# Resident products in TensorE's waits of the first and the last element of a two-layer cross-attention

## The chip, the cores and the metric

One core of a Trainium2 chip. The metric is the device time of one execution in microseconds, the median of several runs.

## What is computed

32 elements (B = 32) pass through two layers of cross-attention with a residual each. An element has 112 queries of 320 channels and a context of 375 positions by 512 channels; there are 20 heads of 16. In the first layer the first 77 context positions ("text") and the rest ("image") have their own softmax and their own key and value weights:

```python
out_text = _merge_heads(_attend(q, k, v, sm_scale))
out_ip = _merge_heads(_attend(q, k_ip, v_ip, sm_scale))
out = (out_text + IP_SCALE * out_ip) @ Wo.T + bo + residual
```

In the second layer the first 371 positions are the text and the last 4 the image; the image scores get a cosine between the attention-weighted context and the four image positions, and a mask by query:

```python
qsem = _l2norm(jnp.einsum('bhst,bte->bhse', probs_t, text_ehs))
sem = jnp.einsum('bhse,bne->bhsn', qsem, ip_n)
probs_ip = softmax(attn_scores + SEM_SCALE * sem) * spatial_mask[None, None, :, None]
out = (text_out + ip_out) @ W_out + b_out + residual
```

## The kernel before, in words

Nothing is scheduled by a tool. `stage_order` (L53) writes one list of stages by hand, and each of the five engines walks through that same list (`tensor` L578, `vector` L837, `scalar` L1041, `gpsimd` L1214, `sync` L1291) and issues its own share of each stage, with waits on semaphores. So a stage's place in the list sets the order on every engine and on SP's DMA queue.

Large products are split in two or three parts of lower precision: keys, values and the Gram matrix of the context run as fp32r products of high and low parts (`k` L583, `v_mm` L651, `g` L666), scores as stacks of bfloat16 parts in one product (`scores` L698). To stay in range each query's maximum over the keys is found first: `s_max` (L677) makes the scores of 3 heads in `ST` (three PSUM banks) or of 2 heads in `PN` (the two banks `PV` and `NS`), VectorE reduces them (L930 to L936), `m_T` (L692) transposes the maxima, GpSimd splits them in three parts (`m_split` L1267), and six (or three) DMAs put them as extra rows into `Qs` (L1419), for which the first `scores` wait. The queries (`q`, L635) and the text keys (L587 to L593) are plain float32 products of 128 weights; a call of `e.matmul` on float32 leaves two records of MATMUL in the profile.

The keys and queries in their parts go to DRAM (`k` L1361, `q` L1397) and come back with the parts stacked (`k_stack` L1386, `q_stack` L1403).

PSUM has three more banks `R0` to `R2` that all small results take in turn: `in_bank` (L58) gives a result the next bank, and `free` (L554) makes TensorE wait until the one that had this bank three results ago was read.

For element b the loop (L286) issues the first layer of element b and the second layer of element b-1, and between them the keys, values and Gram tiles of element b+1, so that TensorE has work while ScalarE makes exponentials and VectorE multiplies. The first element (b = 0) has no second layer of an earlier one to fill its waits, and there the weights are loaded and split as well (`key_weights` L892, `weights` L897). In the last rounds (b = 31 and b = 32) no further element is there: the maxima of the second layer of element 31 (`maxima`, L354, `between` L340), the second layer of element 31 (`groups1` L161), and the chain at its end, `ns_T`, `fuse`, `ip_softmax`, `ip_T`, `ip_mm`, `o_T`, `o_mm`, `out` (`finish1` L204), where each step waits for the one before on another engine. `take` (L229) draws steps from these generators; `finish0` (L190) is the chain `pvT`, `o_T`, `o_mm`, `x1_T`, `q` that ends the first layer.

`wkt` (L406) holds the first layer's text key weights as float32, `[128, 4, 384]`; it is loaded once (L1304) and stays.

Of the kernel before, what the change touches and what calls it, by code (L numbers as in the profile page):

```python
# [6 lines left out]
B, S, C, T, E = 32, 112, 320, 375, 512  # L7
# [21 lines left out]
class Order:  # L29
# [15 lines left out]
    def share(self, buffer, slots, what, signal, value):  # L45
# [3 lines left out]
        self.freed[buffer, what] = ends[len(ends) - slots] if len(ends) >= slots else None  # L49
        ends.append((signal, value))  # L50


def stage_order():  # L53
    o = Order()
# [6 lines left out]
    def flush():  # L61
        now = later[:]
        later.clear()
        for stage in now:
            o.add(*stage)

    def keys(b, l, m):
        o.add("k", b, l, m)
        in_bank(("k", b, l, m), "k_rem", o.at("k", b, l, m))
        o.share("rem", 2, ("k", b, l, m), "k_low", o.at("k", b, l, m))  # L70
# [47 lines left out]
    def maxima(b, l, between):  # L118
        for h in range(0, H, 5):
            for h0, wide in ((h, True), (h + 3, False)):  # L120
                o.add("s_max", b, l, h0, wide)
                if wide:
                    o.share("ST", 1, ("s_max", b, l, h0), "s_max_read", o.at("s_max", b, l, h0, wide))
                else:
                    for part in ("PV", "NS"):
                        o.share(part, 1, ("s_max", b, l, h0), "s_max_read", o.at("s_max", b, l, h0, wide))
                between()
        return m_rows(b, l)
# [100 lines left out]
    def take(pieces, n):  # L229
        for _ in range(n):  # L230
            next(pieces, None)
# [7 lines left out]
    o.add("split", 0)  # L239
    o.add("key_weights", 0)  # L240
    keys(0, "t", 0)
    keys(0, 0, 0)
    o.add("image_keys")
    for m in range(3):
# [9 lines left out]
    o.add("k_stack", 0, 0, 0)  # L254
    o.add("k_stack", 0, 0, 1)
    o.add("q_stack", 0, 0)
    for m in range(2):
        keys(0, 1, m)
    o.add("ctx", 1)
# [1 line left out]
    in_bank("image_values", "vip_copied", 1)  # L261
    in_bank("image_norms", "nip_max", 1)
    o.add("vip_out")
    o.add("text_rest")
    o.add("v_mask")
    o.add("weights", 2)
# [5 lines left out]

    start = with_maxima()
    take(start, 3)
    rows0 = maxima(0, 0, lambda: take(start, 1))
    take(start, 99)
    flush()
    o.add("split", 1)
# [7 lines left out]
    for b in range(B + 1):  # L286
        if b + 1 < B:
            o.add("xT", b + 1)
        pieces = ahead(b) if b < B else iter(())
        first, last = iter(()), iter(())  # L290

        def among0(g):
            take(rows1, 1)
            take(pieces, 1 if b + 1 < B and (b or g < 4) else 0)
            if g < 2:
                flush()

        def among1(g, end):
            if g or not end:
                take(first, 1)  # L300
            if g == 0 and b + 1 < B:
                take(pieces, 1)
            if end and g == 2 and b < B:
                o.add("k_stack", b, 1, 0)

        if not b:
            take(pieces, 2)
        if b < B:
            groups0(b, among0)
            first = finish0(b)  # L310
        else:
            flush()
            flush()
        take(rows1, 9)
        if not b:
            take(pieces, 2)
        if b + 1 < B:
            o.add("k_stack", b + 1, 0, 0)
            o.add("k_stack", b + 1, 0, 1)
            o.add("q_stack", b + 1, 0)  # L320
        if b:
            groups1(b - 1, among1)
            last = finish1(b - 1)
            take(last, 1)
        else:
            o.add("k_stack", b, 1, 0)
        take(first, 99)
        if b < B:
            o.add("k_stack", b, 1, 1)
            o.add("q_stack", b, 1)  # L330
        if not b:
            take(pieces, 3)
        if b + 1 < B:
            o.add("xn", b + 1)
        if b + 2 < B:
            o.add("ctx", b + 2)
        count = [0]
        rows0 = iter(())

        def between():  # L340
            count[0] += 1
            if count[0] > 9:
                take(rows0, 1)
            if count[0] in (1, 2, 3, 5, 7, 9, 10):
                take(last, 1)
            if count[0] in (2, 4, 6, 8, 11, 12, 14, 16):
                take(pieces, 1)
        if b + 1 < B:
            rows0 = maxima(b + 1, 0, between)
            take(rows0, 1)  # L350
        if b + 1 == B:
            take(pieces, 99)
        if b < B:
            rows1 = maxima(b, 1, between)  # L354
            take(rows1, 1)
        take(rows0, 9)
        take(last, 99)
        take(pieces, 99)
    return o

# [24 lines left out]
def xattn_two_layers(nc, a, out):  # L385
# [3 lines left out]
    with ctx:  # L389
# [164 lines left out]
        def free(w, buffer, what):  # L554

            if o.freed[buffer, what]:
                signal, value = o.freed[buffer, what]
                w.wait_ge(freed_by[signal], value)
# [19 lines left out]
        def tensor(e):  # L578
            w = Waiter(e)
            for kind, key in o.stages:  # L580
                if kind == "start":
                    w.wait_ge(pool_set, 1)
                elif kind == "k":  # L583
# [3 lines left out]
                    if l == "t":  # L587
                        w.wait_ge(d_text, 16 * (b // QUAD + 1))
                        w.wait_ge(d_load["wk0"], 16)
                        free(w, "R", ("k",) + key)  # L590
                        for k in range(3):
                            e.matmul(r[:, 0:n], wkt[:, k, c0:c0 + 128], tx[:, k, :], start=k == 0, stop=False)
                        e.matmul(r[:, 0:n], wkt[:, 3, c0:c0 + 128], tx[:, 3, :], start=False, stop=True).then_inc(k_mm, 1)  # L593
                    else:
                        i, t0, t1 = (1, 0, TEXT1 + 1) if l == 1 else (0, TEXT0, T)
                        h, lo, wh, wl = ch[b % 2], cl[b % 2], wkh[i], wkl[i]
                        w.wait_ge(c_low, 4 * (b + 1))
                        w.wait_ge(wk_low, 4 * i + 4)
                        free(w, "R", ("k",) + key)
                        for k in range(4):  # L600
                            e.matmul(r[:, 0:t1 - t0], wh[:, k, c0:c0 + 128], h[:, k, t0:t1], start=k == 0, stop=False)  # L601
                            e.matmul(r[:, 0:t1 - t0], wh[:, k, c0:c0 + 128], lo[:, k, t0:t1], start=False, stop=False)  # L602
                            if k < 3:
                                e.matmul(r[:, 0:t1 - t0], wl[:, k, c0:c0 + 128], h[:, k, t0:t1], start=False, stop=False)  # L604
                        e.matmul(r[:, 0:t1 - t0], wl[:, 3, c0:c0 + 128], h[:, 3, t0:t1], start=False,
                                 stop=True).then_inc(k_mm, 1)
                elif kind == "image_keys":
                    w.wait_ge(d_load["cip"], 16)
                    w.wait_ge(d_load["wkip1"], 16)
# [7 lines left out]
                elif kind == "image_values":  # L617
# [10 lines left out]
                    for k in range(3):  # L628
                        e.matmul(r[:, 0:NI], ones, csq[:, k, :], start=k == 0, stop=False)
                    e.matmul(r[:, 0:NI], ones, csq[:, 3, :], start=False, stop=True).then_inc(nip_mm, 1)  # L630
                    w.wait_ge(d_load["ident"], 16)
                    w.wait_ge(v_mask, 1)
                    w.wait_ge(oT_ones, 1)
                    w.wait_ge(d_load["ones_rows"], 48)
                elif kind == "q":  # L635
                    b, l = key
                    r, rhs = R[slot["R", ("q",) + key]], (xT, x1T)[l]
# [880 lines left out]
```

## Time and profile before

| | |
|---|---|
| runs, median of 3 | 2601.96 us (2598.71 to 2601.97) |
| the profiled execution, its own time | 2602.68 us |
| its span, first to last instruction | 2600.9 us |
| mean granted clock of TensorE | 0.981 |
| TensorE busy | 2476.0 us, 95% of the span, 26280 matmul records |
| VectorE, ScalarE, GpSimd busy | 63%, 47%, 30% |

The profile is one execution. Its page gives busy shares in 40 slices of the span, the granted clock of TensorE in tenths of full speed (0.50 is the lower of its two levels, 1.2 GHz; 1.00 the higher, 2.4 GHz), and the costliest groups of instructions. The order of time shows each instruction's start in us, its duration, and in brackets how long its engine had been idle before it and what ended that. The view by stretches gives for each stretch the busy time of every engine.

### The profile page before, as it was taken

What the parts mean: (1) busy time and instruction counts of PE and PEld (TensorE: products, weight loads), DVE (VectorE), ACT (ScalarE), POOL (GpSimd) and SP (SyncE); (2) the same over time, 40 slices, a digit from 0 to 9 for tenths busy, and PEclk for the clock granted to TensorE, in tenths of its full rate; (3) what the DMA queues carried; (4) which work ended last, traced back from release to release, by engine and by line L of the source; (5) the groups of instructions that cost most, each with busy time, mean ns of one, the idle gap of its engine ahead of it and who ended that gap; (6) DMA issues with size and microseconds to landing.
All of it is one profiled execution on the core that took longest, in us unless ns stands there. A gap on an engine that the chain in (4) does not pass through costs nothing.

```text
span 2600.9 us, 64063 instructions
## 1 busy us (share of the span) xinstructions
PE 2476.0 (95%) x26280; PEld 2127.6 (82%) x26280; DVE 1641.6 (63%) x3217; ACT 1233.5 (47%) x2311; POOL 767.9 (30%) x998
## 2 busy tenths in 40 slices
PE   6789999999999999999999999999999999999996
PEld 5678888888888888888888888888888888888874
DVE  4246776566676566676656676566676656667655
ACT  3344445544445554444554444554444554444543
POOL 2122322322323332332332332332332332333222
PEclk8889999999999999999999999999999999999997
DMA  9855777655677655677655577755577755577630
GB/s 205 110 83 77 111 96 105 82 96 90 91 95 105 93 87 90 88 95 114 93 81 89 87 105 103 95 81 92 95 94 103 95 82 90 83 95 100 89 38 7
DMA packets 493226, 241.46 MB, mean 93 GB/s; under 512 B 259628, under 2 KB 492924, under 8 KB 492925
## 3 DMA queue, kind: packets, MB, share of 16 engines
q1 hardware_dynamic: 492934, 237.37, 62.1%
q8 instruction: 208, 3.41, 0.7%
q14 instruction: 84, 0.68, 0.2%
HBM read 171.35 MB, written 64.59 MB: 91 GB/s over the span
## 4 chain that ended last, share of the span: by engine, by line
PE 77%; DVE 17%; issue 2%; SPq 1%; DMA 1%; ACT 1%; POOL 0%; DVEq 0%; ACTq 0%; POOLq 0%
PE ST L706 7%; DVE w L844 6%; PE PN L723 5%; PE R L750 5%; PE R L648 5%; PE R L661 4%; PE R L662 4%; PE R L601 4%; DVE m L931 4%; PE R L602 4%; PE PN L768 3%; PE R L808 3%; PE R L664 3%; PE R L604 3%; DVE w L841 3%; PE R L753 2%
## 5 line engine op out<-in xcount | busy, mean ns | idle before, releaser
L1155 ACT ACTIVATE p<-ST 128x1344 f32<-128x1344 f32 x320 | 413.7, 1293 | 122.1 <-PE ST L709 117.7
L1284 POOL TENSOR_TENSOR w<-w 128x448 f32<-128x448 f32 (+1 forms) x256 | 331.0, 1293 | 425.4 <-DVE w L841 407.3
L844 DVE SCALAR_TENSOR_TENSOR w<-p,pr 128x1344 f32<-128x1344 f32 x160 | 297.8, 1861 | 173.7 <-ACT pr L1170 161.5
L841 DVE TENSOR_TENSOR rem<-R,kst 128x298 f32<-128x298 f32 (+2 forms) x180 | 89.5, 497 | 454.4 <-ACT kst L1045 454.4
L750 PE MATMUL R<-pr,Gh 128*128 128x448 f32 (+1 forms) x960 | 367.3, 383 | 0.0
L841 DVE TENSOR_TENSOR w<-R,w 128x448 f32<-128x448 f32 (+1 forms) x480 | 281.6, 620 | 70.5 <-PE R L755 60.0
L661 PE MATMUL R<-wvh,ch 128*128 128x320 f32 (+3 forms) x896 | 301.5, 337 | 3.8 <-DVE wvl L841 3.8
L1218 POOL TENSOR_TENSOR kst<-rem,kst 128x298 bf16<-128x298 f32 (+2 forms) x180 | 148.4, 824 | 480.6 <-ACT kst L1045 262.6
L662 PE MATMUL R<-wvh,cl 128*128 128x320 f32 (+3 forms) x896 | 278.4, 311 | 0.0
L706 PE MATMUL ST<-Qs,Ks 100*128 100x112 bf16 (+1 forms) x3520 | 231.1, 215 | 22.2 <-DMA Qs<-ms 12.0
L706 PEld LDWEIGHTS ST<-Qs,Ks 100*128 100x128 bf16 (+1 forms) x3520 | 185.8, 99 | 75.7 <-issue 35.0
L601 PE MATMUL R<-ch,wkh 128*128 128x298 f32 (+1 forms) x640 | 218.7, 342 | 8.5 <-DVE wkl L841 8.5
L1045 ACT ACTIVATE pvt<-PN 128x112 f32<-128x112 f32 (+1 forms) x320 | 98.0, 306 | 250.2 <-PE PN L772 193.8
L664 PE MATMUL R<-wvl,ch 128*128 128x320 f32 (+3 forms) x672 | 208.8, 311 | 0.0
L1170 ACT ACTIVATE pr<-ST 128x1344 fp32r<-128x1344 f32 x160 | 204.9, 1281 | 0.0
L602 PE MATMUL R<-cl,wkh 128*128 128x298 f32 (+1 forms) x640 | 203.5, 318 | 0.0
L750 PEld LDWEIGHTS R<-pr,Gh 128*128 128x128 f32 (+1 forms) x960 | 176.7, 184 | 22.6 <-issue 6.2
L753 PE MATMUL R<-pr,Gl 128*115 128x448 f32 (+1 forms) x480 | 177.0, 369 | 0.0
L755 PE MATMUL R<-pr,Gl 128*128 128x448 f32 (+1 forms) x480 | 176.0, 367 | 0.0
L935 DVE TENSOR_REDUCE m<-ST 112x3 f32<-112x1113 f32 x128 | 167.9, 1312 | 9.2 <-PE ST L690 9.2
L661 PEld LDWEIGHTS R<-wvh,ch 128*128 128x128 f32 (+3 forms) x896 | 162.2, 181 | 9.0 <-issue 4.1
L1045 ACT ACTIVATE V<-R 128x320 f32<-128x320 f32 (+3 forms) x162 | 68.3, 437 | 211.8 <-PE R L665 209.9
(192 smaller groups left out, 5842.0 us busy)
## 6 DMA issues: line engine op xcount, KB each, us to landing
Ks<-k_split SPq DMA_DIRECT2D x384, 140.6 KB, 6.0
Ks<-k_split SPq DMA_DIRECT2D x384, 93.8 KB, 8.3
Qs<-q_split SPq DMA_DIRECT2D x384, 70.0 KB, 8.6
w<-in_ctxT SPq DMA_DIRECT2D x31, 750.0 KB, 6.1
k_split<-kst SPq DMA_DIRECT2D x64, 281.2 KB, 3.5
k_split<-kst SPq DMA_DIRECT2D x64, 223.5 KB
q_split<-qst SPq DMA_DIRECT2D x128, 84.0 KB, 2.5
k_split<-kst SPq DMA_DIRECT2D x62, 111.8 KB, 2.7
```

The source lines that it names most:

```text
L601: e.matmul(r[:, 0:t1 - t0], wh[:, k, c0:c0 + 128], h[:, k, t0:t1], start=k == 0, stop=False)
L602: e.matmul(r[:, 0:t1 - t0], wh[:, k, c0:c0 + 128], lo[:, k, t0:t1], start=False, stop=False)
L661: e.matmul(r[0:n, 0:C], h[:, k, :], wh[:, k, :], start=k == 0, stop=False)
L662: e.matmul(r[0:n, 0:C], lo[:, k, :], wh[:, k, :], start=False, stop=False)
L664: e.matmul(r[0:n, 0:C], h[:, k, :], wl[:, k, :], start=False, stop=False)
L706: e.matmul(ST[:, u, S * h:S * h + S], Ks[l][0:m, GH * g + h, 128 * u:128 * u + 128], Qs[l][0:m, GH * g + h, :], start=True, stop=True)
L750: e.matmul(r[0:nj, 0:QW], Gh[0:ROWS[u], q:q + nj], x[0:ROWS[u], QW * u:QW * u + QW], start=u == 0, stop=False)
L753: e.matmul(r[0:nj, 0:QW], Gl[0:ROWS[u], q:q + nj], x[0:ROWS[u], QW * u:QW * u + QW], start=False, stop=False)
L841: return e.tensor_tensor(to, x, y, op)
L844: return e.scalar_tensor_tensor(out=to, in0=x, scalar=s, in1=y, op0=op0, op1=op1)
L1155: e.activation(p32[i][:].rearrange("p (u q) -> p u q", u=3), st, ACT.Exp).then_inc(p_whole, 1)
L1284: e.tensor_tensor(first, first, w2[n % 2][0:ROWS[j], QW * j:QW * j + QW], ALU.add).then_inc(ns_added, 1)
```

## The change

`Order` gets a method that looks up the next bank of a ring and when it comes free, without taking it. A new stage `warm` makes TensorE multiply a 128 by 128 part of `wkt` with itself n times into columns 384 to 511 of bank `NS` or of the `R` bank that is next in turn; no one reads these columns. The stage is put at 30 places of the list: in the first element 26 calls before the first long keys, 28 before `keys(0, 1, 0)`, 28 before the values (and the waits for constants that stood at the end of `image_values` become a stage behind them), 5, 8, 3, 8, 3 and 14 after the third to the eighth maximum, 18 before the first scores, 6 between the second scores and `k(1, 1, 0)`, 9, 6, 8 and 6 behind the steps of `finish0(0)`, 16 before `s_max(1, 0, 0)`; in the last rounds 16 before `scores(30, 1, 0)`, 6 behind each of the eight maxima of `(31, 1)`, 40 between `m_T(31, 1)` and `scores(31, 1, 0)`, and 30, 4, 8 and 5 behind `ns_T`, `ip_T`, `ip_mm` and `o_T` of element 31. Other engines have nothing to do in these stages.

```diff
+    def borrow(self, buffer, slots, what):
+
+        ends = self.ring.get(buffer, [])
+        self.slot[buffer, what] = len(ends) % slots
+        self.freed[buffer, what] = ends[len(ends) - slots] if len(ends) >= slots else None
+
...
+    def warm(bank, n):
+
+        key = (o.many.get("warm", 0), bank, n)
+        o.add("warm", *key)
+        if bank == "R":
+            o.borrow("R", 3, ("warm",) + key)
...
     keys(0, "t", 0)
+    warm("NS", 26)
     keys(0, 0, 0)
...
     o.add("q_stack", 0, 0)
+    warm("NS", 28)
     for m in range(2):
         keys(0, 1, m)
...
     o.add("vip_out")
+    warm("NS", 28)
+    o.add("constants")
     o.add("text_rest")
...
-    rows0 = maxima(0, 0, lambda: take(start, 1))
+    gaps = iter((0, 0, 5, 8, 3, 8, 3, 14))
+
+    def among():
+        n = next(gaps)
+        take(start, 1)
+        if n:
+            warm("R", n)
+
+    rows0 = maxima(0, 0, among)
...
         def among0(g):
+            if g == 1 and not b:
+                warm("NS", 6)
             take(rows1, 1)
...
         if not b:
             take(pieces, 2)
+            warm("NS", 18)
         if b < B:
             groups0(b, among0)
             first = finish0(b)
         else:
             flush()
             flush()
+            take(rows1, 1)
+            warm("NS", 40)
         take(rows1, 9)
...
+        if b + 1 == B:
+            warm("NS", 16)
         if b:
             groups1(b - 1, among1)
...
-        take(first, 99)
+        for n in (9, 6, 8, 6, 0):
+            take(first, 1)
+            if n and not b:
+                warm("NS", n)
...
         if not b:
             take(pieces, 3)
+            warm("R", 16)
...
             if count[0] in (2, 4, 6, 8, 11, 12, 14, 16):
                 take(pieces, 1)
+            if b + 1 == B:
+                warm("R", 6)
...
-        take(last, 99)
+        for n in (30, 0, 0, 4, 8, 5, 0):
+            take(last, 1)
+            if n and b == B:
+                warm("R", n)
...
+                elif kind == "warm":
+                    _, bank, n = key
+                    w.wait_ge(oT_ones, 1)
+                    if bank == "R":
+                        free(w, "R", ("warm",) + key)
+                    spare = (R[slot["R", ("warm",) + key]] if bank == "R" else NS)[:, 384:512]
+                    for _ in range(n):
+                        e.matmul(spare, wkt[:, 0, 0:128], wkt[:, 0, 0:128], start=True, stop=True)
+                elif kind == "constants":
+                    w.wait_ge(d_load["ident"], 16)
+                    w.wait_ge(v_mask, 1)
+                    w.wait_ge(d_load["ones_rows"], 48)
...
-                    w.wait_ge(d_load["ident"], 16)
-                    w.wait_ge(v_mask, 1)
-                    w.wait_ge(oT_ones, 1)
-                    w.wait_ge(d_load["ones_rows"], 48)
```

## Rows read from the trace of the kernel before

**Rows 1.** The page, granted clock of TensorE in 40 slices of the span.
```profile
PEclk8889999999999999999999999999999999999997
```

**Rows 2.** Stretches of both elements: length; PE, PEld, DVE, ACT, POOL busy; clock; DMA.
```profile
7.10:11.30 4.20, 4.18 (x8) 2.51 (x8) 0.00 (x0) 2.11 (x4) 0.23 (x1) 1.00 1.08 377
11.30:16.20 4.90, 0.02 (x1) 0.00 (x0) 3.55 (x5) 2.98 (x8) 3.92 (x4) 0.81 0.95 298
16.20:21.10 4.90, 4.85 (x21) 4.88 (x22) 1.08 (x3) 0.88 (x2) 0.91 (x2) 0.50 0.09 13
...
36.10:41.70 5.60, 5.57 (x18) 5.57 (x19) 0.55 (x1) 0.83 (x2) 0.00 (x0) 0.50 0.78 202
...
50.20:55.20 5.00, 4.99 (x19) 4.79 (x20) 1.26 (x1) 0.44 (x1) 0.00 (x0) 0.50 1.33 129
...
2499.40:2502.70 3.30, 3.30 (x11) 2.67 (x10) 1.33 (x3) 0.63 (x1) 1.14 (x1) 0.51 0.02 5
...
2558.20:2567.50 9.30, 6.69 (x36) 5.79 (x36) 2.81 (x3) 4.94 (x4) 0.99 (x1) 0.50 0.05 11
...
2590.50:2597.90 7.40, 5.73 (x12) 2.46 (x12) 0.49 (x1) 0.76 (x3) 0.00 (x0) 0.56 0.00 0
```

**Rows 3.** First element, order of time on TensorE: start, duration, instruction, count, idle before.
```profile
16.25 0.58 PE L601 MATMUL R<-ch,wkh 128*128 128x298 f32 x1 [4.93 <-DVE wkl L841]
...
30.38 1.95 PE L648 MATMUL R<-xT,wq 128*128 128x128 f32 x16
...
36.13 0.68 PE L601 MATMUL R<-ch,wkh 128*128 128x372 f32 x1 [3.58 <-DVE wkl L841]
...
50.21 0.52 PE L661 MATMUL R<-wvh,ch 128*77 128x320 f32 x1 [3.75 <-DVE wvl L841]
...
63.04 0.50 PE L688 MATMUL ST<-Ks,Qs 96*112 96x375 bf16 x2 [0.86 <-DVE m L931]
...
68.53 0.35 PE L697 MATMUL R<-ident_sb,m 112*40 112x112 f32 x1 [1.57 <-DVE m L931]
...
76.55 1.21 PE L706 MATMUL ST<-Qs,Ks 102*128 102x112 bf16 x11 [2.67 <-DMA Qs<-ms]
...
88.42 0.72 PE L706 MATMUL ST<-Qs,Ks 102*128 102x112 bf16 x11 [3.04 <-ACT p L1155]
```

**Rows 4.** The query stack's tile, 44 to 60 us: reads, first maximum, landing times.
```profile
L1409 SPq DMA_DIRECT2D Qs<-q_split x6: 429/840/1823, 45.7 to 49.8; - x6
...
L688 PE MATMUL ST<-Ks,Qs x2: 323/324/325, 57.8 to 58.0; 96*112 96x375 bf16 x2
...
DMA to landing us min/median/max: 7.9/8.7/9.0
```

**Rows 5.** Order of time, 84 to 165 us: TensorE, GpSimd, SP's queue.
```profile
108.84 0.38 PE L799 MATMUL R<-ident_sb,o 112*128 112x112 f32 x2 [0.98 <-DVE o L841]
...
113.54 2.05 PE L648 MATMUL R<-x1T,wq 128*128 128x128 f32 x16 [0.59 <-ACT x1T L1045]
...
117.53 0.83 POOL L1218 TENSOR_TENSOR qst<-qrem,qst 128x336 bf16<-128x336 f32 x1 [16.07 <-DVE qst L922]
...
119.55 3.18 SPq L1401 DMA_DIRECT2D q_split<-qst  x3
```

**Rows 6.** Last rounds, order of time on TensorE.
```profile
2494.61 0.71 PE L706 MATMUL ST<-Qs,Ks 100*128 100x112 bf16 x11
...
2497.94 0.71 PE L706 MATMUL ST<-Qs,Ks 100*128 100x112 bf16 x11 [2.29 <-ACT pr L1170]
...
2547.93 0.60 PE L799 MATMUL R<-ident_sb,o 112*128 112x112 f32 x2 [0.28 <-DVE o L841]
...
2558.24 1.21 PE L706 MATMUL ST<-Qs,Ks 100*128 100x112 bf16 x11 [5.21 <-DMA Qs<-ms]
...
2590.49 0.27 PE L828 MATMUL R<-ident_sb,fus 112*80 112x112 f32 x1 [3.93 <-DVE fus L844]
...
2594.34 2.47 PE L808 MATMUL R<-wo,x1T 128*112 128x320 f32 x4 [0.59 <-ACT x1T L1045]
```

## Prediction, before any run of the changed kernel

> **What bounds the kernel now.** I read the page first: TensorE is the busiest engine by far, and its granted clock is at the high level (2.4 GHz) in all slices but the first three and the last [rows 1]. So the middle of the kernel is TensorE at full speed, where the change puts nothing; there is time to win only where the clock is low and TensorE's work is on the path. Then I read the granted clock by stretches of the first and the last element [rows 2]. After each long wait it stands at 0.50 (1.2 GHz) and real products run at half speed: 4.85 us of them in 16.2 to 21.1, 5.57 in 36.1 to 41.7, 4.99 in 50.2 to 55.2, 3.30 in 2499.4 to 2502.7, 6.69 in 2558.2 to 2567.5, 5.73 in 2590.5 to 2597.9. Half of each is what a high clock would give back. Last I read the order of time on TensorE for the waits themselves: 4.93, 3.58, 3.75, 2.67, 3.04 us in the first element [rows 3], and 2.29, 5.21, 3.93 in the last [rows 6].
>
> **What one added product costs.** Each `warm` product is float32, 128 weights wide by 128 columns, like those of the query stage: there 8 calls leave 16 records, so one call is two passes. 16 passes take 1.95 us with the latency of the last one [rows 3], some 0.111 us a pass; the text keys, 308 columns, take 4.18 us for 8 passes at the low speed [rows 2], 0.217 for 128 columns, 0.108 at the high one. Both say 0.22 us a call at the high clock and 0.44 at the low. The diff adds 192 calls in the first element and 151 in the last, 76 us of TensorE at the high clock. A call isn't free just because it stands in a wait: TensorE takes its stream in order, so what a group is longer than its wait delays the product behind it.
>
> The Trainium skill (TensorE: Matmul & The Clock Gate, "Back-to-back issue gap") gives about 56 ns for a 128-column product at the high clock; at that price all 343 calls would be 19 us, every group would fit its wait, and the time would be that of the first rival below. The float32 rows here show two passes of 0.111 us, so the trace doesn't bear it out for this type.
>
> **First element, by hand.**
> Group of 26 (before the first long keys): the first eight products ran at the low price, yet the record falls to 0.50 only within 11.3 to 16.2 [rows 2], so the clock had risen by then; I take the calls at the high price. 26 x 0.22 = 5.8 us against a wait of 4.93: +0.9. Behind it 4.85 us of low-clock work gives back 2.2. Net -1.3 at the image keys.
> Group of 28: it begins 1.3 earlier, lasts 6.2, and the wait was 3.58 [rows 3]: the keys start 1.3 later than now, though their split weights come 1.3 earlier. Their 24 passes, nearly all at the low clock, give back 2.7: net -1.4.
> Group of 28 before the values: 6.2 against 3.75, so +1.0 there, and 2.3 back from 4.99 us: net -1.3. The stack of queries that the maxima need is issued last at 49.8 and lands 7.9 to 9.0 us later [rows 4], just when the maxima start (57.8 [rows 4]); its chain is also 1.3 earlier, no more.
> Maxima (41 calls in six groups, 9.1 us): now VectorE sets the pace and TensorE has short waits, as the 0.86 at 63.04 [rows 3]. After the second maximum (59.2 in the changed kernel) come 15 products of 0.16 us (spacing of [rows 3]), 2.4 us, and 9.1 us of calls: TensorE is never free before 70.9, and the transpose of the maxima starts then instead of at 68.53 [rows 3]: +2.3. All that hangs on it (split of the maxima, six DMAs on SP, the first scores) moves as one: 76.55 becomes 78.9. The group of 18 (4.0 us) fits into what is left of that wait, since the keys before it run fast.
> 88.42: the wait of 3.04 us ends with a key write that is queued on SP behind those DMAs; it moves too. The group of 6 ends before that wait, which grows longer, so the clock falls there again. Cost between 0 and 1.3 us of more low-clock work; I take 0.6.
> 29 calls between the steps of the output projection: 6.4 us in four waits, the first 0.98 and the last 0.59 [rows 5], 2.9 together. Group by group (2.0, 1.3, 1.8 and 1.3 us, each counted from the end of the step's passes) the second queries start 2.9 later. Their low part is ready at 118.4 (0.83 us from 117.53) and SP takes it at 119.55 [rows 5]: 1.2 us of slack, at most 1.7 left. I take 1.2, as the DMA behind it may land sooner when fewer others are under way. The group of 16 (3.6 us) stands before maxima that are due long before the second element's first scores, whose DMA chain sets the time: nothing.
> The waits that stood before `constants` move behind 28 calls; their loads had landed long before: nothing. `borrow` waits for the next bank, which was read long before in each place: nothing.
> First element: 2.3 + 0.6 + 1.2 = **+4.1**. Bounds: 0 if SP and the DMAs hide most, +7 if the clock falls more often.
>
> **Last element.**
> Group of 16 before the scores at 2494.61: these have no wait now [rows 6]; the wait of 2.29 comes behind them, at 2497.94. So the whole group, 3.6 us, is a delay. It may save the dip of 2499.4 to 2502.7, worth 1.5; the wait behind the scores is still there, so I give it half: +2.8 (bounds 2.1 and 3.6). TensorE is the bound from there on.
> Eight groups of 6 (10.7 us) between the maxima, which VectorE paces: by steps of 1.33 us the sixth maximum is 0.6 late, the seventh 1.1, and the output's transpose (2547.93) 2.7 [rows 6]. The projection behind it takes 3.55 us at the low clock (like the one at 2594.34, where 4 of the 6 passes are 2.47 [rows 6]), 1.8 less at the high, the transpose 0.3 less: +0.5 behind it.
> Group of 40: 8.9 us behind the last maxima's transpose, where the wait before the scores at 2558.24 is 5.21 and 0.4 more is the transpose's own record [rows 6]: +3.3. The 6.69 us of low-clock work behind it give 3.3 back, if the clock holds over 2.5 us of ScalarE; half a chance of losing 1.5: +0.7 (bounds 0 and 1.5).
> The end: 30 calls, 6.7 us, where the wait is 3.93 and some 0.15 of the record ahead of it can be used [rows 6]: the transpose at 2590.49 moves by +2.6. Groups of 4, 8 and 5 (0.9, 1.8, 1.1 us) stand in waits of 0.6 or so, as the 0.59 at 2594.34: with the faster products between them +0.9 more, so 2594.34 becomes 2597.8. The projection at the high clock gives back 1.8: **+1.7** at the end, past which nothing can hide.
> Last element: 2.8 + 0.5 + 0.7 + 1.7 = **+5.7** (4.2 to 7.3).
>
> Sum: +9.8 on the profiled execution's 2602.68 is 2612.5; the median of the runs shown is 0.7 lower, so **2611.8**. Of the gains of the high clock some 15 us are real and counted; the groups' overhang eats them and more.
>
> **Rivals.**
> *Groups fit, faster.* If a call costs 0.13 us or less, nothing overhangs. For it: 30 calls in 3.93, 28 in 3.58, 28 in 3.75 and 40 in 5.21 us all come to 0.13 a call, as if laid out for that. Against it: no float32 product here has one pass, and the passes' spacing. The point that decides is the last transpose: above 0.131 us a call 2590.49 moves out. It gives -3 in the first element (DMAs and VectorE hold the rest), -1 at 88, then +2.1 - 1.5, -2.5, -3.3 and -2.8: -11, 2591. Chance with other ways to a gain: 0.24.
> *DMAs and SP hide it, same.* The first element's delays fall into the slack of SP's queue, so about 0 there, and the last element comes to its lower bound of 4: 2606; or up to 2 us more are gained in each. Chance 0.22.
> *The clock doesn't rise at 11.3.* Then 26 calls cost 11.4 us and push everything 5 us further: 2617. Chance 0.06, inside slower.
> *The overhang as summed*, 0.48.
>
> **How the numbers follow.** A measurement of this kernel tells 0.2% (5.2 us) from no change. Slower by more: 0.48 + 0.06 = 0.54. Within: 0.22. Faster: 0.24. The likeliest case alone is 2607 to 2616. The range runs from 2591, the rival on the other side, to 2619, the sum of the upper bounds with a little of the low-clock case.
>
> **What would show it.** In the changed profile: two records per call, 0.11 apart; the mean clock above 0.98; the first long keys near 17.1, the transpose of the first maxima near 70.9, first scores near 78.9; in the tail no idle time of TensorE before its last transpose, but 30 calls of 6.7 us before it, 6.5 us after the one before; the last projection in 1.7 us. If the transpose stays 4 us behind the one before, the price is wrong and the rival is right. If the tail is late as summed but the first scores of the second element aren't, the DMAs hid the rest.

## The result and the profile after

| | before | changed kernel |
|---|---|---|
| median of 5 runs each, one series | 2598.71 us (2595.71 to 2601.97) | 2612.23 us (2609.87 to 2613.23) |
| ratio, 95% interval | | 1.0049 [1.0038, 1.0061] |
| profiled execution, its span | 2602.68, 2600.9 us | 2612.48, 2610.7 us |
| mean granted clock of TensorE | 0.981 | 0.995 |
| TensorE busy, matmul records | 2476.0 us, 26280 | 2524.3 us, 26966 |

The clock was held nearly everywhere, and the kernel is slower. The 686 new records are the 343 calls at two passes each. The page of the changed kernel (its granted clock answers to [rows 1]), and its groups by form of the new line, with total busy time and mean of one record:

```profile
PE 2524.3 (97%) x26966; PEld 2188.6 (84%) x26966; DVE 1641.6 (63%) x3217; ACT 1233.8 (47%) x2311; POOL 767.7 (29%) x998
...
PEclk9999999999999999999999999999999999999999
...
L655 PE MATMUL PN<-wkt 128*128 128x128 f32 x382 | 44.6, 275 | 0.0
...
L655 PE MATMUL R<-wkt 128*128 128x128 f32 x304 | 37.0, 275 | 0.0
```

The 275 ns are one record with its latency; 60 records take 6.86 us below, 0.111 us a pass with one latency at the end. So a call is 0.22 us, as taken. The view by stretches of the same kernel (length, busy time of each engine, clock, DMA), which answers to [rows 2]:

```profile
11.30:17.00 5.70, 5.70 (x52) 5.67 (x51) 3.85 (x5) 3.45 (x10) 4.17 (x4) 1.00 0.89 276
17.00:21.70 4.70, 4.70 (x40) 4.67 (x39) 2.12 (x6) 1.37 (x5) 1.53 (x2) 1.00 0.10 17
...
90.00:96.00 6.00, 5.92 (x23) 4.52 (x24) 0.90 (x2) 2.29 (x5) 1.09 (x2) 0.50 0.35 86
2500.00:2515.00 15.00, 12.66 (x110) 10.65 (x109) 7.05 (x11) 6.88 (x8) 2.27 (x2) 0.89 0.00 1
2569.30:2576.50 7.20, 4.64 (x62) 3.79 (x59) 3.29 (x5) 4.95 (x4) 1.00 (x1) 1.00 0.01 2
2595.00:2610.70 15.70, 12.73 (x103) 11.66 (x102) 3.22 (x11) 3.11 (x7) 0.00 (x0) 1.00 0.03 9
```

What was at 0.50 in [rows 2] now runs at 1.00, but for the dip within 2500 to 2515. Four stretches are still low: the one behind the wait of 4.27 us at 90.08, the one behind the wait of 5.86 us at 155.64 (no group stands in it), 2489 to 2492, where the waits are only 0.49 us and the kernel before isn't low (it costs 0.7 us), and that dip. What holding the clock cost is in the order of time on TensorE (start, duration, count, idle before), first element, which answers to [rows 3 to 5]:

```profile
11.32 5.97 PE L655 MATMUL PN<-wkt 128*128 128x128 f32 x52
17.05 0.39 PE L642 MATMUL R<-ch,wkh 128*128 128x298 f32 x1
...
30.95 6.42 PE L655 MATMUL PN<-wkt 128*128 128x128 f32 x56
37.12 0.42 PE L642 MATMUL R<-ch,wkh 128*128 128x372 f32 x1
...
67.31 3.29 PE L655 MATMUL R<-wkt 128*128 128x128 f32 x28
70.44 0.26 PE L746 MATMUL R<-ident_sb,m 112*40 112x112 f32 x1
73.88 4.18 PE L655 MATMUL PN<-wkt 128*128 128x128 f32 x36
78.37 0.71 PE L755 MATMUL ST<-Qs,Ks 102*128 102x112 bf16 x11 [0.31 <-DMA Qs<-ms]
...
90.08 1.21 PE L755 MATMUL ST<-Qs,Ks 102*128 102x112 bf16 x11 [4.27 <-ACT p L1204]
...
119.35 1.95 PE L697 MATMUL R<-x1T,wq 128*128 128x128 f32 x16
...
155.64 1.21 PE L755 MATMUL ST<-Qs,Ks 102*128 102x112 bf16 x11 [5.86 <-DMA Qs<-ms]
```

The waits of 4.93, 3.58 and 3.75 us are gone; in their places stand groups that last longer than they did. The transpose of the maxima is 1.9 us later (68.53 before), the first scores 1.8 (76.55), the second queries 5.8 (113.54), the second element's first scores 2.75 (152.89). The last rounds of the changed kernel in the same view, which answer to [rows 6]:

```profile
2494.21 0.71 PE L755 MATMUL ST<-Qs,Ks 102*128 102x112 bf16 x11
2498.08 3.84 PE L655 MATMUL PN<-wkt 128*128 128x128 f32 x32
2501.75 0.71 PE L755 MATMUL ST<-Qs,Ks 100*128 100x112 bf16 x11
2505.07 0.71 PE L755 MATMUL ST<-Qs,Ks 100*128 100x112 bf16 x11 [2.34 <-ACT pr L1219]
...
2560.36 9.11 PE L655 MATMUL PN<-wkt 128*128 128x128 f32 x80
2569.31 0.71 PE L755 MATMUL ST<-Qs,Ks 100*128 100x112 bf16 x11
...
2594.50 6.86 PE L655 MATMUL R<-wkt 128*128 128x128 f32 x60
2601.20 0.26 PE L877 MATMUL R<-ident_sb,fus 112*80 112x112 f32 x1
...
2605.95 1.24 PE L857 MATMUL R<-wo,x1T 128*112 128x320 f32 x4
```

The lag against before grows as follows: 3.5 us where the group of 16 begins (0.7 of it from the low stretch at 2489), 7.1 behind it (2494.61 became 2501.75), 7.6 at the transpose ahead of the group of 40 (2552.64 became 2560.26), 11.1 behind that group, 8.1 after the fast products that follow (2586.24 became 2594.34), 10.7 at 2601.20, 11.6 at the last projection, 9.8 at the end.

### The profile page after: what moved, and what is told of

Its sections match the earlier page's. It is cut to its first block, busy times and chain, and to the rows that moved or that the text cites. A ratio compares the mean times of both kernels' runs of the same rounds, so it can differ in the third digit from the quotient of the medians.

```text
span 2610.7 us, 65429 instructions
## 1 busy us (share of the span) xinstructions
PE 2524.3 (97%) x26966; PEld 2188.6 (84%) x26966; DVE 1641.6 (63%) x3217; ACT 1233.8 (47%) x2311; POOL 767.7 (29%) x998
## 4 chain that ended last, share of the span: by engine, by line
PE 79%; DVE 16%; issue 1%; DMA 1%; ACT 1%; SPq 1%; POOL 0%; DVEq 0%; POOLq 0%; ACTq 0%
PE ST L755 7%; DVE w L893 6%; PE PN L772 5%; PE R L799 5%; PE R L697 5%; PE R L710 4%; PE R L711 4%; PE R L642 4%; DVE m L980 4%; PE R L643 4%; PE PN L817 3%; PE R L713 3%; PE R L857 3%; PE R L645 3%; DVE w L890 3%; PE ST L737 2%
## 5 line engine op out<-in xcount | busy, mean ns | idle before, releaser
L1267 POOL TENSOR_TENSOR cl<-w,ch 128x375 fp32r<-128x375 f32 x124 | 110.4, 922 | 192.1 <-ACT ch L1094 192.1
```

Source lines behind the costliest of these rows:

```text
L1267: return e.tensor_tensor(to, x, y, ALU.subtract)
```

## The experiments

Each ratio below is against the kernel before in the same series, 6 to 12 runs against 15 to 33, and a difference in us is read from the ratio; e9 (2604.61 us) and e10 (2614.64 us) are one execution each. A **split of each trace** runs through all of them: the second element's first scores (155.64 in the rows above), the last scores of element 31's first layer (2494.21, the last rows with 102x112), and the end of the span.

| kernel | to the first mark | between | from the second mark to the end |
|---|---|---|---|
| before | 152.9 | 2337.9 | 110.2 |
| changed | 155.6 | 2338.6 | 116.5 |
| e1, first element only | 151.2 | 2341.0 | 110.1 |
| e2, last element only | 148.2 | 2336.7 | 118.0 |
| e3, half of every group | 152.3 | 2339.1 | 104.0 |
| e4, bfloat16 calls | 151.0 | 2339.2 | 106.2 |
| e5, without the group of 16 | 151.1 | 2338.9 | 112.8 |
| e6, last element, half, no 16 | 149.2 | 2338.8 | 105.1 |
| e7, e6 and ten calls behind the scores | 148.2 | 2341.6 | 103.6 |
| e8, fitted | 151.2 | 2336.1 | 102.1 |
| e9, the 41 calls of the maxima cut to 13 | 146.4 | 2338.4 | 118.0 |
| e10, the 29 calls of the projection cut to 11 | 153.5 | 2341.4 | 118.0 |
| e11, fitted, no new places in the first element | 152.7 | 2336.4 | 102.0 |
| e12, fitted, last element only | 153.2 | 2337.6 | 103.2 |

The last column follows the groups to 1.5 us. The first two don't: before, e2, e6, e7 and e12 have the same first element, and its length there is 148.2 to 153.2. The changed kernel, e1 and e5 have the same one too, with all its groups: 155.6, 151.2 and 151.1. The two ranges overlap, so the first mark of a trace doesn't show what the groups cost there. Two stretches inside the first element do repeat. From the first maxima to their transpose it is 14.1 us in the changed kernel, e1, e5 and e10, and 10.6 to 11.0 in the five without groups; from the second `pvT` (at 102.48 before) to the second queries it is 13.9 us in the changed kernel, e1, e5 and e9, and 11.1 in those five, but for 12.6 in e12. At the first mark, behind the DMAs that follow, the difference is within the spread.

### The two halves of the change

e1 keeps the first element's groups alone, e2 the last one's:

```diff
     def warm(bank, n):
 
+        if o.many.get("ip_T", 0) or o.many.get("scores", 0) > 20:
+            return
```

> Only the first element's groups. Overhang theory: the marks of the changed kernel's trace stand 2.75 us late at the second element's first scores and 3.5 us late at 2494.6 of before, so this kernel is 2.7 to 3.5 us slower than before. Rival (the middle of the kernel also suffers from something the change does): more than that, up to the whole 9.8. Rival (DMAs hide the first element, the marks are noise of one execution): within 1 us of before.

```diff
+        if o.many.get("scores", 0) < 20:
+            return
```

> Only the last element's groups. Overhang theory: 9.8 - 3.5 = 6.3 us slower than before, of which 3.55 at the group of 16, 0.5 at the maxima, 3.45 less 3.0 around the group of 40, 1.7 in the last chain. Rival (something other than the groups' length): not the sum of these, or less than 4.

e1: 2604.77 against 2600.6 us, 1.0013 [1.0004, 1.0021], or 3.4 us. e2: 2607.11, 1.0022 [1.0013, 1.0031], 5.7 us. Both parts cost, the last element more, as expected. Their sum, 9.1 us, is a little below the whole's interval (9.9 to 15.9 us); the upper ends of the two intervals add to 13.5, so no effect of one part on the other needs to be assumed.

### Half the counts

```diff
+        n = n // 2
```

> Every group at half its calls (171 calls or so, 38 us). Overhang theory: all groups but the one of 16 fit their waits, so the clock's gains stay: last element -8 (2.1 at the group of now 8 given back by the dip or not), first element -3 to -4, in all 9 to 12 us faster than before, 2587 to 2591. Rival (the held clock brings nothing, since DMAs and VectorE set the path): within 3 us of before. Rival (each call costs whatever its place): about +5, half of the loss.

2596.97 us, 0.9986 [0.9976, 0.9995]: 3.6 us faster (1.3 to 6.2) where 9 to 12 were expected; the time alone doesn't rule out the first rival's 3 us. The sign turned, so the overhang is what made the change slow. The table says where the rest stayed: the last element gained 6.2 us (110.2 to 104.0), the first 0.6. The order of time of e3 around its first maxima, and two of its stretches:

```profile
56.46 0.85 PE L738 MATMUL ST<-Ks,Qs 96*112 96x375 bf16 x2 [5.43 <-DMA Qs<-q_split]
```

```profile
54.00:60.00 6.00, 3.54 (x13) 3.38 (x14) 1.39 (x2) 0.00 (x0) 0.00 (x0) 0.65 1.12 210
88.00:96.00 8.00, 7.46 (x50) 6.04 (x54) 1.38 (x3) 3.44 (x7) 2.02 (x5) 0.66 0.27 67
```

TensorE comes to the values 4.65 us earlier than before (45.56 for 50.21), has done those ahead of the maxima at 51.0, and then waits 5.43 us for the query stack to land. The clock falls in that wait, and the maxima's transpose starts at 69.33 (68.53 before). What is gained ahead of a transfer is lost at it.

The last element of e3 shows what a fitted group does at the end:

```profile
2583.37 3.51 PE L656 MATMUL R<-wkt 128*128 128x128 f32 x30
2587.38 0.29 PE L878 MATMUL R<-ident_sb,fus 112*80 112x112 f32 x1 [0.49 <-DVE fus L894]
...
2590.59 1.33 PE L858 MATMUL R<-wo,x1T 128*112 128x320 f32 x4
```

Fifteen calls end 0.49 us before the transpose can go, and the projection still runs fast: 1.33 us, against 2.47 in [rows 6].

### Calls at a quarter of the price

A bfloat16 tile of ones, 128 by 128, takes the place of the float32 weights, counts unchanged:

```diff
+        wb = sb("wb", [128, 128], bf16)
-                        e.matmul(spare, wkt[:, 0, 0:128], wkt[:, 0, 0:128], start=True, stop=True)
+                        e.matmul(spare, wb[:], wb[:], start=True, stop=True)
```

> The same 343 calls, but on a bfloat16 tile of ones of its own (one memset on VectorE more), one pass each. Overhang theory: 0.056 to 0.08 us a call, 19 to 27 us in all, no group overhangs; but a group now covers a quarter to a third of its wait, so it depends on whether that holds the clock: held everywhere 11 us faster, held nowhere within 1 us of before or 1 slower from the group of 16. Rival (the number of added instructions costs, not their length): as slow as the changed kernel, or half of it since each call leaves one record instead of two.

2600.36 us, 1.0002 [0.9992, 1.0012]: no difference. The order of time and the stretches at its first group:

```profile
11.45 1.86 PE L658 MATMUL PN<-wb 128*128 128x128 bf16 x26
16.34 0.59 PE L644 MATMUL R<-ch,wkh 128*128 128x298 f32 x1 [3.04 <-DVE wkl L893]
```

```profile
11.30:16.30 5.00, 2.01 (x27) 1.68 (x25) 3.56 (x5) 3.08 (x8) 4.01 (x4) 0.91 0.98 306
16.30:21.00 4.70, 4.66 (x20) 4.69 (x21) 1.07 (x3) 0.88 (x2) 0.77 (x1) 0.50 0.09 14
```

One record a call; in the last element of this trace 16 calls take 1.07 us and 40 take 2.40, so one is 0.055 us. The Trainium skill (TensorE: Matmul & The Clock Gate, "Back-to-back issue gap") gives about 56 ns for a product alone and about 81 in a stream with weight loads; the trace's 0.055 agrees with the first. So the price is one of the type, and the price the prediction refused is right for bfloat16 calls. Here the groups are too short: 3.04 us of idle time are left, and the keys behind run at 0.50 again. A group must cover its wait nearly to the end, not only fit into it. In the last element that still left 4.0 us of gain; in the first, the later keys ran fast (1.00 in 36 to 41, behind 2.02 us of idle time) and the values in part (0.50 in 50 to 52), but TensorE then waited 3.87 us for the query stack (maxima at 59.13), and at the first mark nothing is left that could be told from the spread.

### The last element, step by step

e5 is the changed kernel without the group of 16:

```diff
-        if b + 1 == B:
-            warm("NS", 16)
```

> The changed kernel without the one group of 16 ahead of the scores of element 30 that had no wait. Overhang theory: the whole 3.6 us come back, 0.14% below the changed kernel, so about 1.0035 of before; the dip of the clock after the next wait stays as it is, since it was there with the group too. Rival (the group pays for part of itself by the clock): less than 2 us come back.

2609.34 us against 2603.77, 1.0028 [1.0017, 1.0038]. Its tail is 112.8, 3.7 less than the changed kernel's: the group of 16 costs all of its 3.6 us and returns nothing, for the clock falls behind the next wait with it and without it. The third scores of element 30's second layer come 7.5 us after the second in the changed kernel (2505.07) and in e5 alike.

That isn't a matter of the place alone. e3 has eight calls and e4 16 bfloat16 ones at the same place, ahead of the scores, and there the clock holds through the same wait. The second and third scores in e3:

```profile
2500.45 0.71 PE L756 MATMUL ST<-Qs,Ks 100*128 100x112 bf16 x11 [2.34 <-ACT pr L1220]
...
2506.37 0.70 PE L756 MATMUL ST<-Qs,Ks 100*128 100x112 bf16 x11
```

5.9 us, also in e4: the eight calls cost 1.9 us and gave 1.5 back. In the four traces with the 16 float32 calls (changed, e2, e9, e10) and the four with none there (before, e1, e5, e6) it is 7.5. Why is open: two traces are few, and other waits keep the clock in one execution and lose it in the next (last section).

e6 drops the first element's groups and that of 16, and halves the rest; e7 puts ten calls into the wait behind the scores instead:

```diff
+        if o.many.get("scores", 0) < 20:
+            return
+        n = n // 2
...
             between(g, False)
+            if g == 0 and b == B - 2:
+                warm("NS", 20)
```

(The last two lines are in e7 alone; halved, they are ten.)

> Only the last element's groups, at half their calls, and none of 16: nothing overhangs. Overhang theory, from the marks of the kernel with all groups at half: 8.0 us faster than before (0.9969), 2.5 of it at the maxima and the projection behind them, 3.0 to 3.3 behind the group of now 20, 2.4 in the last chain. Rival (it was the first element that brought the half kernel's gain): within 2 us of before.

> The same with 10 calls put behind the scores of element 30, into their wait of 2.3 us. If this wait is what lets the clock fall 1.5 us later: 1.5 us faster than the kernel without them, 0.9963 of before. Rival (the fall comes from the shorter waits before): no gain.

e6: 2595.31 us, 0.9974 [0.9963, 0.9985]. e7: 2594.86, 0.9968 [0.9959, 0.9978]. Both came as expected. With the ten calls the third scores come 5.9 us after the second, where it is 7.5 in e6, and the tail is 1.5 us shorter; in the ratios that step is too small to be told.

### Every group sized by its wait

e8 gives each group as many calls as its wait holds at 0.22 us, and adds groups where e3 still waited:

```diff
-    warm("NS", 26)
+    warm("NS", 20)
...
-    warm("NS", 28)
+    warm("NS", 15)
...
-    warm("NS", 28)
+    warm("NS", 16)
...
-    gaps = iter((0, 0, 5, 8, 3, 8, 3, 14))
+    gaps = iter((0, 0, 1, 3, 0, 3, 0, 6))
+    warm("NS", 22)
...
-            if g == 1 and not b:
-                warm("NS", 6)
+            if g == 2 and not b:
+                warm("NS", 18)
...
+        if b == 1:
+            warm("R", 13)
...
-            warm("NS", 40)
+            warm("NS", 22)
...
-        for n in (9, 6, 8, 6, 0):
+        for n in (4, 2, 3, 2, 0):
...
-            warm("R", 16)
+            warm("R", 8)
...
-                warm("R", 6)
+                warm("R", 3)
...
+            if not b:
+                warm("R", 12)
...
-        for n in (30, 0, 0, 4, 8, 5, 0):
+        for n in (16, 0, 0, 2, 3, 2, 0):
```

The ten calls of e7 are in it and the group of 16 is not.

> The last element as in the kernel before this one, and in the first element groups of the length that the half kernel's trace shows (20, 15, 16; 22 ahead of the first maxima, where it waits 5.4 us for the query stack; 1, 3, 3, 6 among them; 18 more ahead of the third scores, 12 and 13 in the two waits before the second element's scores). If a held clock is worth something there: 2 to 4 us faster than the last element alone, 0.995 of before; of it 1.5 to 2 by the second element's first products. If DMAs and VectorE set that path: no more than 1 us.

2589.58 us (2588.6 to 2594.32) against 2603.77, **0.9956 [0.9943, 0.9968]**: faster than both kernels, by 11.5 us than the one before. Its stretches, and its order of time at the first maxima and at the end:

```profile
90.00:96.00 6.00, 4.68 (x38) 4.13 (x38) 1.38 (x3) 4.06 (x7) 2.05 (x4) 1.00 0.36 87
...
2494.00:2508.00 14.00, 13.94 (x153) 11.75 (x153) 9.08 (x11) 7.44 (x13) 4.55 (x4) 1.00 0.00 1
```

```profile
50.92 5.07 PE L660 MATMUL PN<-wkt 128*128 128x128 f32 x44
57.21 0.50 PE L742 MATMUL ST<-Ks,Qs 96*112 96x375 bf16 x2 [1.22 <-DMA Qs<-q_split]
...
2577.41 3.74 PE L660 MATMUL R<-wkt 128*128 128x128 f32 x32
2581.42 0.29 PE L882 MATMUL R<-ident_sb,fus 112*80 112x112 f32 x1 [0.27 <-DVE fus L898]
```

Two of the stretches that the change left low are at 1.00, and the last long group ends 0.27 us before the transpose. Not every wait is filled: 1.22 us are left ahead of the first maxima and 2.19 ahead of the second element's first scores (151.23), and behind the wait of 2.56 us in element 31's last scores the clock still falls (0.72 in 2554 to 2560). Two further versions ask which part of it counts. e11 is e8 without the four groups new in the first element (22, 18, 12 and 13 calls); e12 is e8 with no group in the first element at all:

```diff
+        if o.many.get("scores", 0) < 40:
+            return
```

> The fitted version without the four groups that the change did not have in the first element (22 before the first maxima, 18 before the third scores, 12 and 13 before the second layer's maxima); all other sizes as fitted. Theory (size alone was wrong, places were right): a ratio of 0.9965 or below, as most of the fitted version's gain is in the last element, some 2 us above the fitted version. Rival (the new places in the first element carry the gain over half counts): 0.998 or above, as for half counts.

> The fitted version without any group in the first element; the last element as fitted. In every trace so far the last element is as long as its groups make it, to 1.5 us: from the last first-layer scores of element 31 to the end 110.16 us before, 102.1 and 102.0 in the two fitted versions, so 102 here and a ratio of 0.9969 (8.1 us). For the first element, theory one (its waits end by DMAs and SP, the groups give nothing there): the second element's first scores start between 148 and 153 us, as in the four traces with that first element, and the time is within 2 us of the fitted versions' mean of 8 us below before. Theory two (a held clock in the first element is worth the 3 us by which the fitted version beat 8): this kernel stays at 0.9969, and the first scores come later than the fitted version's 151.23, at 152.9 as before.

e11: 2593.93 us against 2599.27, 0.9983 [0.9974, 0.9992]. e12: 2595.43 against 2601.81, 0.9975 [0.9966, 0.9985]. e11's number is the rival's, but its reason isn't: e12 has fewer groups still and is no slower. The tails are 102.1, 102.0 and 103.2, 7 to 8 us below before, in all three; e12's 1.2 more were not expected, and 1.1 of them lie behind that wait of 2.56 us, where the third scores of element 31's second layer come 6.5 us after the second, against 5.4 to 5.5 in e8 and e11. Of e12's theories none is singled out: its 6.5 us lie within 2 of 8, as theory one has it, and the interval (3.9 to 8.8) holds theory two's 8.1 as well; its first scores at 153.15 are where theory two had them and 0.15 past the end of theory one's range. What the last element gives is the solid part: with fewer calls there, the tails of e3, e6, e7, e8, e11 and e12 are 5.1 to 8.2 us shorter than before's, and e6, e7 and e12, which change nothing else, are 6.5 to 8.3 us faster. Whether the first element's groups give e8 another 3 us, or cost e11 as much, isn't settled: the two were not in one series, and the first element's own spread is larger.

### Two groups of the first element by themselves

e9 and e10 are the changed kernel with one line of e8 each:

```diff
-    gaps = iter((0, 0, 5, 8, 3, 8, 3, 14))
+    gaps = iter((0, 0, 1, 3, 0, 3, 0, 6))
```

> The changed kernel with 13 calls among the first maxima instead of 41. Theory (the 9.1 us of calls held TensorE, not the maxima's own work): the transpose of the maxima starts at 68.7 or earlier instead of 70.44, the first scores at 76.7 instead of 78.37, and the second element's first scores 1 to 1.8 us before 155.64. Rival (DMAs and SP behind the transpose set the path): the transpose is earlier, but the second element's first scores stay within 0.5 us of 155.64.

```diff
-        for n in (9, 6, 8, 6, 0):
+        for n in (4, 2, 3, 2, 0):
```

> The changed kernel with 11 calls between the steps of the first output projection instead of 29. Up to 100 us nothing moves. Theory (18 calls of 0.22 us are 4 us, of which the waits never held 2.9): the second queries start at 116 to 117 instead of 119.35, SP writes the split queries at 121.5 to 122.5 instead of 124.09, and the second element's first scores come 1.2 to 2 us before 155.64. Rival (SP's own queue or its DMAs set this path): SP's write moves by less than 0.5 us and so do the scores.

The order of time of e9:

```profile
56.22 0.48 PE L737 MATMUL ST<-Ks,Qs 96*112 96x375 bf16 x2
...
66.69 0.28 PE L746 MATMUL R<-ident_sb,m 112*40 112x112 f32 x1 [0.35 <-DVE m L980]
...
74.81 0.71 PE L755 MATMUL ST<-Qs,Ks 102*128 102x112 bf16 x11 [0.43 <-DMA Qs<-ms]
...
146.43 1.21 PE L755 MATMUL ST<-Qs,Ks 102*128 102x112 bf16 x11 [2.17 <-DMA Qs<-ms]
```

From the first maxima to their transpose it takes 10.5 us, about as before (10.7, 57.83 to 68.53), where the changed kernel takes 14.1 (56.32 to 70.44). So the 41 calls cost 3.6 us there, and the first scores follow one to one (74.81 for 78.37). That bears out the theory up to 75 us. The 9.2 us at 146.43 are more than the 28 calls last in all (6.2), so some of them are the spread of this element; against e1 and e5, which have all 41 calls, it is 4.7. Of e10 the stretch that it changes, TensorE's rows and then SP's queue:

```profile
103.97 0.51 PE L786 MATMUL R<-ident_sb,pvt 128*112 128x128 f32 x3 [0.82 <-ACT pvt L1094]
...
115.05 2.05 PE L697 MATMUL R<-x1T,wq 128*128 128x128 f32 x16
```

```profile
121.91 1.77 SPq L1450 DMA_DIRECT2D q_split<-qst  x3
```

From the transpose to the second queries it is 11.1 us, as before (102.48 to 113.54), against 13.9 in the changed kernel (105.42 to 119.35): the 29 calls cost 2.9 us. But 1.4 us of e10's lead were there at its start, so at SP's write (121.91 for 124.09) only 0.7 of the 2.9 are left. SP holds this path for most of it, which is the rival's mechanism, though the write moved by more than the rival's 0.5. The second element's first scores came 2.15 us earlier (153.49), with the theory, but within the spread too, and the whole was 2.2 us longer than the changed kernel's profiled execution: 2.8 more between the marks, where the code is the same, and 1.5 more behind them.

## Why the prediction was right, and where it was off

Predicted 2611.8 us and slower; measured 2612.23. The level agrees better than the difference: +9.8 stood on an execution of 2602.68, which is high for the kernel before, while the medians differ by 13.5, the ratio gives 12.7 (9.9 to 15.9), and the two profiled executions differ by 9.8. Against the medians the sum is 3.7 us too small and the base 3.3 too high; that they cancel to 0.4 is luck.

- **What one added product costs:** right, 0.22 us. e4 shows that at 0.055 the kernel isn't slower.
- **Group of 26, both groups of 28:** the first long keys at 17.05 (predicted 17.1, from 16.25), the clock up from 11.3 on, against the rival of a low clock. e3 shows their excess was real, and that removing it helps little, as the query stack's landing comes next.
- **Maxima:** predicted 70.9 (its terms, 59.2, 2.4 and 9.1, add to 70.7) and 78.9, measured 70.44 and 78.37. The overhang was 3.4 us (14.1 against 10.7) rather than 2.3, since the maxima started 1.5 us earlier (56.32, not 57.8).
- **88.42:** the clock fell there as said, at 1.7 us of lag; with the low products behind it I took 0.6 and the write of keys on SP was 3.0 late (101.48 to 104.44), 1.3 more than at 90.08. Undersized by 0.7.
- **29 calls in the output projection:** 2.9 us as summed (e10), and the second queries' low part reached SP 4.5 us later than before (119.55 to 124.09). At the second element's first scores 2.75 us were left (155.64), with a DMA as releaser; predicted 4.1. The 2.75 are no confirmation: e1 and e5, with the same first element, have their first scores at 151.2 and 151.1, ahead of before's 152.89. What bears out a cost is e1's ratio, 3.4 us (1.0 to 5.5).
- **Group of 16:** the step that was mis-sized. "I give it half" came out as nothing: 3.6 us, not 2.8 (e5). The wait is behind the scores, as the prediction said, and the clock fell there in all four traces with this group. That a group ahead of them can never hold it isn't shown: in e3 and e4 shorter ones did.
- **Eight groups of 6:** +0.5 predicted, 7.14 to 7.62 measured. **Group of 40:** +3.3 predicted, 3.45 measured, and 3.0 given back: +0.4. "Half a chance of losing 1.5" was apt: with the same code in e2, e9 and e10 the clock falls in the 2.56 us wait on ScalarE behind the first scores, and their tails are 118.0 instead of 116.5.
- **The end:** +1.7 predicted, 8.1 to 9.8 measured.

Of the rivals, *groups fit, faster* had the wrong price, and its terms add to -12.0 and 2590, not -11 and 2591; but its time was near what fitted groups give (2589.6 to 2595.4), for another reason: the gain that can be shown is the last element's, and the 3 us that the rival took from the first are in no trace. *DMAs and SP hide it* was wrong for the last element; in the first, how much of the 3.5 us at the maxima and the 2.9 at the projection is hidden behind the DMAs stays open within the spread.

## What to carry to other kernels

An engine that takes its stream in order pays for every call by which a filler group outlasts its wait, so size each group by (the wait) / (the price of a call read from the same type in the trace), a little below it, and put it into the wait itself: ahead of the instruction before it, 16 calls cost 3.6 us and gave nothing and eight cost 1.9 and gave 1.5, while ten in the wait gave 1.5 for nothing. A held clock is worth half of the low-clock work only where TensorE then sets the end; where a transfer lands next, as in the first element here, the time goes into that wait, and the clock falls there instead. Judge such a change by stretches between marks, and look first at how much the same stretch differs between executions of unchanged code.

## What was not expected of the hardware

- The first element's length spreads over 5 us for the same code. The second element's first scores start at 152.9 in the kernel before; the same row in e7 and in e12:

```profile
148.16 1.21 PE L758 MATMUL ST<-Qs,Ks 102*128 102x112 bf16 x11 [6.38 <-DMA Qs<-ms]
```

```profile
153.15 1.21 PE L762 MATMUL ST<-Qs,Ks 102*128 102x112 bf16 x11 [4.89 <-DMA Qs<-ms]
```

All five end a wait of 4.2 to 6.7 us on a DMA. In e7 and e12 the first maxima wait for the query stack (1.96 and 1.68 us), in before, e2 and e6 they don't. The stretch between the marks, which no edit touches but for its first microseconds, spreads by 5.6 us too; why isn't known.
- The same wait on ScalarE, 2.56 us with TensorE idle, lowers the clock in some executions and not in others (with the same code around it, in e2, e9 and e10 but not in the changed kernel and e5), at a cost of 1.5 us. In all other traces but these two the clock is low behind it, in the fitted ones too, where it costs 1.5 to 2.6 us: a group of its own there was not tried. The stretch behind it in e5 and in e2 (PE busy, ..., clock):

```profile
2564.00:2572.00 8.00, 7.26 (x80) 6.04 (x84) 6.04 (x8) 5.89 (x6) 3.93 (x3) 1.00 0.01 2
```

```profile
2563.00:2571.00 8.00, 7.62 (x68) 6.30 (x69) 5.64 (x7) 4.46 (x6) 3.44 (x2) 0.79 0.01 2
```

- 26 bfloat16 calls in 1.86 us ahead of an idle time of 3.04 us didn't keep the clock up for the keys behind (0.50 in 16.3 to 21.0).
